# Graph attention whose row shifts are made by groups of tiles, without a common barrier before it, and whose late tiles wait for their own edge columns

## The chip, the cores and the metric

One Trainium2 chip, one of its cores. The metric is the device time of one execution in microseconds. A core has five instruction queues that run side by side and meet only by semaphores: PE (matrix products), DVE (vector), ACT (scalar, with function tables), POOL (GpSimd) and SP (here it only issues DMAs and reads registers).

## What is computed

Two layers of a graph network on 1250 nodes with 512 channels and 40000 edges. The part of the change is the sparse multi-head attention of the first layer (8 heads of 64):

```python
s = jnp.einsum('ehd,ehd->eh', q[src], k[dst]) / np.sqrt(D) + att_bias
m = jax.ops.segment_max(s, src, num_segments=n)
p = jnp.exp(s - m[src])
denom = jax.ops.segment_sum(p, src, num_segments=n)
alpha = p / jnp.where(denom[src] == 0, 1.0, denom[src])
agg = jax.ops.segment_sum(alpha[:, :, None] * v[dst], src, num_segments=n)
att = agg.reshape(n, C) @ Wo.T + bo
```

The edges come sorted by `dst`. The kernel works densely: `exp(q k - shift)` over all pairs of nodes, times a table in HBM that holds for each pair (dst, src) the sum of `exp(att_bias)` of its edges and their count. The shift of a source and head is its largest score over all nodes, with the sign turned and 40 added; any shift gives the same quotient.

## The kernel before

**Edge table.** Edge number n lies in column n // 128, 313 columns in all. `edges_pool` (from L610) adds one column after the other to the HBM table with an indirect DMA (L623), at most two in flight. The two semaphores `s_scat` count the landed even and odd columns. DVE makes the columns ready eight at a time ("turns": `mark` and `settle`, with PE's `spread_line` and `sum_repeats` and ACT's `copy_row`), a turn or two in each tile of the stages before. POOL does nothing but these scatters until they are all issued.

**Projections** (`gnn_pe`, `gnn_act`, `gnn_dve`, from L1101): ten tiles of 125 nodes, each with three products (q, k, v), their evictions on DVE (L1125), the transposes of q and k (copied by ACT, L1195 and L1196), and in the first six tiles two turns of edge work each. In tiles 0 to 4 PE spreads the first half of the next turn's keys before the transposes and the second half after them, which needs the first half copied by ACT (L412); ACT copies it behind the two copies of q and k. After the ten tiles DVE reads how many columns the first five tiles of `dst` need (`needed_columns_dve`, L644 to L647; the counting itself, L633 and L635, is in the tenth tile), adds the output bias to all ten tiles of `XN` (L1143), and builds constants (L1145 to L1154).

**Maxima.** 120 units of PE products (L1269) in four pairs of PSUM banks, each reduced by DVE (L1160): 12 units a tile, two of 512 columns and one of 226 for each of four pairs of heads. When all are done, DVE makes the shifts of all tiles (L1163, L1165), PE turns them (L1275), ACT copies them into `shiftT` (L1206), and PE, ACT and DVE call `leave_stage`, each waiting for the other two.

**Attention.** 50 blocks (5 chunks of 250 sources for the destination tiles 0 to 4, then again for tiles 5 to 9) of two units each, 100 units. For a unit, PE makes scores (L1550, L1556: the second adds the shift), ACT the exponentials in place (L1529, which needs the table of Exp), DVE multiplies them by the table's block (L1450), PE multiplies by the values (L1571), and a sum over a pass's weights is added up (L1486) by DVE in the first five passes and by POOL, behind the last scatter in its queue, in the other five. `att_sp` (from L1369) loads three blocks ahead into a ring of three slots (L223, L224, six DMAs and 1.1 MB each). Before the first it waits for the barrier, reads two registers (L651, L652) and waits for the columns that tiles 0 to 4 need (`soon_filled`); before block 25 it waits for all 313 (`table_filled`). Within a loop round i it waits for a_cc (counts copied), stores two small pieces of the adjacency, waits until block i is multiplied, and loads block i + 3. The place of the ring's third slot still holds edge values that the scatters read, so among the first 25 blocks the third of every three uses a slot of its own, `aside`.

## Time and profile before

| | us |
|---|---|
| median of 3 runs | 2275.96 |
| lowest and highest of them | 2274.62, 2282.95 |
| the profiled execution | 2270.11 |
| its span in the trace | 2268.0 |
| PE busy, DVE busy, ACT busy, POOL busy | 2064.1, 1348.2, 726.7, 730.7 |
| projections, about | 390 to 543 |
| maxima | 543 to 664 |
| between the last maximum and the first block multiplied | 664 to 679 |
| attention | 679 to about 1020 |

The profiled execution takes 2.1 us more than its span. The busy share of PE (91%) is a mean over stages: in the maxima and in the first half of the attention, PE waits for DVE. What an edit is worth is read from the waits of its own stretch. An instruction of POOL that issues a scatter is over when it is issued; its data land later. L-numbers are lines of the kernel before.

### The profile page before, as it was taken

How to read it: one execution, taken by the hardware profiler on the slowest of the kernel's cores; microseconds unless marked ns; L12 is line 12 of the kernel's file. 1: busy time of each engine (PE TensorE's matmuls, PEld its weight loads, DVE VectorE, ACT ScalarE, POOL GpSimd, SP SyncE). 2: the span in 40 equal slices, each digit the busy share in tenths (PEclk: the TensorE clock that was granted, in tenths of full speed). 3: DMA queues.
4: the chain of work that ended last, by engine and by line, in shares of the span. 5: the costliest groups of instructions: out<-in, count | busy, mean ns of one | idle time of the engine just before them, and what ended most of it. 6: DMA issues, size and time to landing. Idle time of an engine off the chain costs nothing.

```text
span 2268.0 us, 31396 instructions
## 1 busy us (share of the span) xinstructions
PE 2064.1 (91%) x11980; PEld 1260.4 (56%) x11980; DVE 1348.2 (59%) x3189; ACT 726.7 (32%) x1551; POOL 730.7 (32%) x508
## 2 busy tenths in 40 slices
PE   4998986888978898989999999999999999999977
PEld 3555554443325555546764457678677754455554
DVE  6665687877979997752224544341222243289997
ACT  4221122321015554422213355554111111135552
POOL 1346878887875635530000000000000000014443
PEclk9998998999999999999999999999999999999989
DMA  9994232223239987653000010004000014000000
GB/s 324 387 375 118 3 77 3 3 3 66 3 43 214 216 222 219 179 141 126 1 1 10 1 76 1 1 1 171 16 1 1 1 36 117 0 1 10 10 15 14
DMA packets 122053, 181.97 MB, mean 80 GB/s; under 512 B 67761, under 2 KB 69451, under 8 KB 118071
## 3 DMA queue, kind: packets, MB, share of 16 engines
q1 hardware_dynamic: 76833, 178.51, 24.9%
q0 software_dynamic: 45072, 1.46, 5.6%
q8 instruction: 95, 1.56, 0.3%
q14 instruction: 53, 0.43, 0.1%
HBM read 109.21 MB, written 70.71 MB: 79 GB/s over the span
## 4 chain that ended last, share of the span: by engine, by line
PE 58%; DVE 17%; POOL 11%; issue 5%; ACT 4%; DMA 3%; SPq 2%; DVEq 0%; PEldq 0%; ACTq 0%; POOLq 0%; PEld 0%
PE banks L204 17%; POOL edge_table L623 11%; PE banks L2400 6%; PE banks L2442 6%; DVE arena L1450 4%; PE banks L1751 3%; PE banks L2228 2%; PE banks L2216 2%; PE banks L2203 2%; PE banks L1550 2%; PE banks L2826 2%; DMA edge_table<-arena 2%; PE banks L2252 2%; PE banks L1571 2%; PE banks L198 2%
## 5 line engine op out<-in xcount | busy, mean ns | idle before, releaser
L623 POOL DMA_INDIRECT edge_table<-arena x313 | 525.4, 1678 | 256.6 <-DMA edge_table<-arena 153.6
L204 PE MATMUL banks<-arena 128*125 128x512 f32 x1200 | 554.9, 609 | 15.4 <-DVE arena L3046 14.3
L204 PEld LDWEIGHTS banks<-arena 128*125 128x125 f32 x1200 | 221.4, 193 | 261.1 <-issue 243.9
L2853 POOL CAST arena<-arena 125x128 f32<-125x128 uint32 x10 | 2.9, 292 | 699.3 <-DVE arena L2989 699.2
L1450 DVE TENSOR_TENSOR arena<-banks,arena 125x1000 f32<-125x1000 f32 x100 | 193.6, 1952 | 36.6 <-ACT banks L1529 19.7
L2348 DVE SCALAR_TENSOR_TENSOR arena<-banks,arena 125x512 f32<-125x512 f32 x80 | 60.1, 751 | 189.4 <-PE banks L2442 189.4
L2095 DVE CUSTOM_DVE_ANT_0 arena<-banks,arena 125x512 f32<-125x512 f32 (+8 forms) x144 | 73.0, 553 | 128.9 <-PE banks L2203 126.1
L2400 PEld LDWEIGHTS banks<-arena 128*128 128x128 f32 x1280 | 144.0, 192 | 6.7 <-issue 6.6
L1550 PE MATMUL banks<-arena 64*125 64x250 f32 x800 | 113.2, 402 | 37.1 <-DVE arena L1450 33.5
L2400 PE MATMUL banks<-arena 128*128 128x125 f32 x1280 | 146.4, 276 | 0.1
L2442 PE MATMUL banks<-arena 128*125 128x512 f32 x320 | 139.2, 593 | 0.0
L1529 ACT ACTIVATE banks<-banks 125x1000 f32<-125x1000 f32 x100 | 98.8, 988 | 123.4 <-PE banks L1556 117.2
L1486 POOL TENSOR_TENSOR arena<-arena 125x1000 f32<-125x1000 f32 x40 | 95.3, 2401 | 96.2 <-DVE arena L1450 96.2
L1269 PE MATMUL banks<-arena 64*125 64x512 f32 (+1 forms) x480 | 111.0, 564 | 8.0 <-DVE arena L1160 6.5
L1550 PEld LDWEIGHTS banks<-arena 64*125 64x125 f32 x800 | 69.2, 186 | 78.2 <-DVE arena L1450 54.1
L1160 DVE TENSOR_REDUCE arena<-banks 125x2 f32<-125x1024 f32 (+1 forms) x120 | 112.0, 1017 | 0.0
L2367 ACT ACTIVATE arena<-banks,arena 128x125 f32<-128x125 f32 x160 | 45.1, 368 | 203.2 <-PE banks L2400 203.2
L1571 PE MATMUL banks<-arena 125*64 125x250 f32 x800 | 107.3, 389 | 0.4 <-DVE arena L1450 0.4
L2061 POOL MEMSET arena<- 128x1250 f32 x1 | 1.1, 1141 | 315.7 <-PEq L148 315.7
L198 PE MATMUL banks<-arena 125*128 125x125 f32 x560 | 83.4, 281 | 21.3 <-DMA arena<-L_mix_Wv 6.7
L2442 PEld LDWEIGHTS banks<-arena 128*125 128x125 f32 x320 | 59.3, 188 | 74.0 <-issue 74.0
L198 PEld LDWEIGHTS banks<-arena 125*128 125x128 f32 x560 | 64.4, 145 | 52.5 <-issue 24.3
(372 smaller groups left out, 3394.0 us busy)
## 6 DMA issues: line engine op xcount, KB each, us to landing
edge_table<-arena SPq DMA_DIRECT2D x23, 2304.0 KB, 26.2
arena<-edge_table SPq DMA_DIRECT2D x100, 326.8 KB
arena<-edge_table SPq DMA_DIRECT2D x50, 330.8 KB
arena<-L_ffn_W SPq DMA_DIRECT2D x4, 2048.0 KB, 10.2
adjacency<-arena SPq DMA_DIRECT2D x50, 109.4 KB
arena<-adjacency SPq DMA_DIRECT2D x10, 546.9 KB
edge_table<-arena POOLq DMA_INDIRECT x313
arena<-edge_table SPq DMA_DIRECT2D x100, 37.9 KB
```

The lines of the kernel that those rows point to most:

```text
L198: last = nc.tensor.transpose(dst[:, k, :], src[:, k * 128:(k + 1) * 128], ident[0:TP, 0:TP])
L204: last = nc.tensor.matmul(dst, xT[:, i, :], w[:, i, 0:n], start=(i == 0), stop=(i == k - 1))
L623: pool.indirect_dma_start(d["table"], bass.IndirectOffsetOnAxis(ap=cell[0:EP, c:c + 1].bitcast(U32), axis=0), vals[0:EP, c * ROW:(c + 1) * ...
L1160: nc.vector.tensor_reduce(by_part_max[:, t, j, :, u % 3], both[:, :, 0:b - a], AX_X, ALU.max).then_inc(g_mx, 1)
L1269: last = nc.tensor.matmul(bank(2 * (u % 4) + e)[0:TP, 0:b - a], qT_g[64 * e:64 * e + 64, j, tok(t)], kT_g[64 * e:64 * e + 64, j, a:b], sta ...
L1450: nc.vector.tensor_tensor(weights_of(m).rearrange("p (s e n) -> p s e n", s=2, e=2), unit_scores(m).rearrange("p e (s n) -> p s e n", s=2) ...
L1486: ops.tensor_tensor(total_p, total_p, weights_of(m), ALU.add).then_inc(a_sum, 1)
L1529: nc.scalar.activation(unit_scores(m), unit_scores(m), ACT.Exp).then_inc(a_e, 1)
L1550: nc.tensor.matmul(bank(at + e)[0:TP, CHUNK * s:CHUNK * (s + 1)], kT_g[64 * e:64 * e + 64, 2 * h + s, tok(b)], qT_g[64 * e:64 * e + 64, 2 ...
L1571: last = nc.tensor.matmul(bank(h)[64 * e:64 * e + 64, CHUNK * s:CHUNK * (s + 1)], V_g[0:TP, b, DH * head:DH * (head + 1)], weights_of(m)[: ...
L2400: last = nc.tensor.matmul(bank(2 + n % 3)[:, m * TP:(m + 1) * TP], w1_e[a // 2][:, k, (c % 8) * 128:(c % 8 + 1) * 128], yT[:, k, tok(t)], ...
L2442: last = nc.tensor.matmul(bank(5 + n % 3)[0:TP, :], hT_e[t % 2][:, 2 * e + c, :], w2_e[e // 4][:, 2 * (e % 4) + c, :], start=(c == 0), sto ...
```

## The change

It touches five places.

1. **No barrier.** DVE, PE and ACT leave the stage with `pass_stage`, which counts and doesn't wait. SP no longer waits for the barrier. PE's first scores wait for the maxima that have read their banks instead; ACT loads the table of Exp with a dummy instruction.
2. **Shifts in three groups** (tiles 0 to 3, 4 to 7, 8 and 9). DVE makes a group's shifts right behind its last maximum; PE turns the first two groups four units later, in a pair of banks that is skipped for that round, and the last one behind the scores of units 0 and 1; the same on ACT.
3. **First blocks early.** SP waits only for the register values and for the columns of tiles 0 to 4, then loads blocks 0 to 2.
4. **Own columns for late tiles.** Four counts are made instead of one (for 5, 6, 7 and 8 tiles of `dst`). Blocks 25, 26, 27 wait for the columns of tile 5, 6, 7; block 28 waits for all. Blocks 26 and 29 go to `aside`.
5. **Work moved on DVE and ACT.** The counting goes from the tenth projection tile to the start of the first stage (behind `settle(dve, 0)`), the bias of `XN` from behind the ten tiles into each tile, and ACT copies the first half of the next turn's keys ahead of q and k.

```diff
@@ count_columns_dve, now called in mix_dve behind settle(dve, 0)
-            link(dve, nc.vector.scalar_tensor_tensor(out=away[0:EP, 0:USED], in0=key[0:EP, 0:USED], scalar=SOON_KEY,
-                                                     in1=pair_of[0:EP, 0:USED], op0=ALU.is_lt, op1=ALU.mult))
-            nc.vector.tensor_reduce(pairs_needed[0:EP, 0:1], away[0:EP, 0:USED], AX_X, ALU.max).then_inc(s_need, 1)
+            for w, key_bound in enumerate(SOON_KEYS):
+                link(dve, nc.vector.scalar_tensor_tensor(out=src_f[0:EP, 0:USED], in0=key[0:EP, 0:USED], scalar=key_bound,
+                                                         in1=pair_of[0:EP, 0:USED], op0=ALU.is_lt, op1=ALU.mult))
+                link(dve, nc.vector.tensor_reduce(pairs_needed[0:EP, w:w + 1], src_f[0:EP, 0:USED], AX_X, ALU.max))
+            nc.vector.tensor_copy(pairs_needed[0:EP, 4:8], pairs_needed[0:EP, 0:4]).then_inc(s_need, 1)
@@ soon_filled
+        def soon_filled(sp, w):
+            if w == 0:
+                sp.wait_ge(s_need, 4)
+            even = nc.sync.value_load(needed_even[:, w:w + 1], min_val=1, max_val=ALL_EVEN)
+            odd = nc.sync.value_load(needed_odd[:, w:w + 1], min_val=1, max_val=ALL_ODD)
             sp.wait_ge(s_scat[0], even)
             sp.wait_ge(s_scat[1], odd)
@@ gnn_dve
+                nc.vector.tensor_tensor(XN[0:TP, t, :], XN[0:TP, t, :], bo_g[0:TP, :], ALU.add)
             needed_columns_dve(dve)
-
-            for t in range(TILES):
-                nc.vector.tensor_tensor(XN[0:TP, t, :], XN[0:TP, t, :], bo_g[0:TP, :], ALU.add)
...
+                for group in SHIFT_TILES:
+                    if u + 1 == PER_TILE * group.stop:
+                        n = slice(HEADS * group.start, HEADS * group.stop)
+                        dve.wait_ge(g_mx, u + 1)
+                        link(dve, nc.vector.tensor_reduce(
+                            shift_g[0:TP, n], part_max[0:TP, :].rearrange("p (h c) -> p h c", c=3)[:, n, :], AX_X, ALU.max))
+                        nc.vector.tensor_scalar(shift_g[0:TP, n], shift_g[0:TP, n], -1.0, MARGIN, ALU.mult,
+                                                ALU.add).then_inc(g_shift, 1)
+            pass_stage(dve, "DVE")
@@ gnn_act
+                early = gnn_turns[t + 1][:-1] if t + 1 < TILES else ()
+                for k in early:
+                    copy_row(act, 2 * k)
                 act.wait_ge(g_tqk, t + 1)
...
+            for b in range(2):
+                copy_shifts(act, b)
+            nc.scalar.activation(degree_parts[0:TP, 63:64], ident[0:TP, 0:1], ACT.Exp)
+            pass_stage(act, "ACT")
@@ gnn_pe
+                for b_shift, at in enumerate(SHIFT_AT):
+                    if u == at:
+                        pe.wait_ge(g_mx, u - 3)
+                        turn_shifts(pe, b_shift)
+                    if u == at + 3:
+                        pe.wait_ge(g_shift, 3 * b_shift + 3)
@@ att_sp
-            sp.wait_ge(s_stage, 6)
-            soon_filled(sp)
+            soon_filled(sp, 0)
...
-                if i == BLOCKS // 2:
+                late = i - BLOCKS // 2
+                if 0 <= late < len(SOON_KEYS) - 1:
+                    soon_filled(sp, late + 1)
+                if late == len(SOON_KEYS) - 1:
                     table_filled(sp)
@@ att_pe
-            pe.wait_ge(g_shift, 3)
...
+                else:
+                    pe.wait_ge(g_mx, 1 + max(u for u in range(len(MAX_UNITS)) if 2 * pair_of_unit(u) == at))
+                if g < CHUNKS and n == 0 and h == 0:
+                    pe.wait_ge(g_shift, 3 * (tok(2 * c + 1).start // TP // 4) + 3)
```

On DVE, from the tenth projection tile's last eviction to the first block multiplied (the names in brackets are the semaphores that a row waits for), before:

```order
L1125 TENSOR_TENSOR arena<-banks,arena 125x512 [waits gnn_projected]
L644 TENSOR_REDUCE arena<-banks 1x1 [waits columns_needed_step]
L645 TENSOR_SCALAR arena<-arena 1x1 [waits dve_step]
L646 TENSOR_SCALAR arena<-arena 1x1 [waits dve_step]
L647 TENSOR_SCALAR arena<-arena 1x1
L1143 TENSOR_TENSOR arena<-arena 125x512 x10
...
L1160 TENSOR_REDUCE arena<-banks 125x2 [waits gnn_row_scores_ready] x120
L1163 TENSOR_REDUCE arena<-arena 125x80 [waits gnn_partial_maxima_ready]
L1165 TENSOR_SCALAR arena<-arena 125x80 [waits dve_step]
L1450 TENSOR_TENSOR arena<-banks,arena 125x1000 [waits att_exponentials_ready,table_block_loaded_0,stage_left]
```

and in the changed kernel:

```order
L1166 TENSOR_TENSOR arena<-banks,arena 125x512 [waits gnn_projected]
L1180 TENSOR_TENSOR arena<-arena 125x512
L650 TENSOR_REDUCE arena<-banks 1x4 [waits columns_needed_step]
...
L1197 TENSOR_REDUCE arena<-banks 125x2 [waits gnn_row_scores_ready] x48
L1203 TENSOR_REDUCE arena<-arena 125x32 [waits gnn_partial_maxima_ready]
L1205 TENSOR_SCALAR arena<-arena 125x32 [waits dve_step]
...
L1197 TENSOR_REDUCE arena<-banks 125x2 [waits gnn_row_scores_ready] x24
L1203 TENSOR_REDUCE arena<-arena 125x16 [waits gnn_partial_maxima_ready]
L1205 TENSOR_SCALAR arena<-arena 125x16 [waits dve_step]
L1488 TENSOR_TENSOR arena<-banks,arena 125x1000 [waits att_exponentials_ready,table_block_loaded_0]
```

Nine of the ten additions to `XN` have left this place, two of the three small shift pairs stand among the maxima, and the first multiplication no longer waits for the stage.

On SP, in front of the first block's six DMAs, before (`table_block_loaded` is what they raise):

```order
L1370 DMA arena<-L_gnn_Wo 128x2048 [waits repeats_summed]
L651 TENSOR_LOAD arena [waits columns_needed_step,stage_left]
L651 ISA x2
L652 TENSOR_LOAD arena
L652 ISA x2
L223 DMA arena<-edge_table 112x756 [waits columns_scattered_0,columns_scattered_1]
```

and in the changed kernel, there and in front of block 25 (the same stands in front of blocks 26 and 27):

```order
L1406 DMA arena<-L_gnn_Wo 128x2048 [waits repeats_summed]
L658 TENSOR_LOAD arena [waits columns_needed_step]
L658 ISA x2
L659 TENSOR_LOAD arena
L659 ISA x2
L223 DMA arena<-edge_table 112x756 [waits columns_scattered_0,columns_scattered_1]
...
L223 DMA adjacency<-arena 112x2x125 [waits att_counts_copied]
L224 DMA adjacency<-arena 13x2x125
L658 TENSOR_LOAD arena [waits att_weights_ready]
```

The wait for the stage is gone from the first read of a register, and pairs of such reads stand ahead of three late blocks.

On PE, between the last maximum's products and the attention's third unit, before:

```order
L1269 MATMUL banks<-arena 125x226
L1275 MATMUL banks<-arena 8x125 [waits gnn_shift_step]
L1275 MATMUL banks<-arena 8x125 x9
L1550 MATMUL banks<-arena 125x250 [waits gnn_shift_step,gnn_out_weights_loaded,stage_left]
...
L1621 MATMUL banks<-arena 125x512 x3
L1550 MATMUL banks<-arena 125x250 [waits att_weights_ready]
```

and in the changed kernel:

```order
L1311 MATMUL banks<-arena 125x226
L1593 MATMUL banks<-arena 125x250 [waits gnn_shift_step,gnn_partial_maxima_ready,gnn_out_weights_loaded]
...
L1081 MATMUL banks<-arena 8x125 [waits gnn_shift_step]
L1081 MATMUL banks<-arena 8x125
L1667 MATMUL banks<-arena 125x512 x3
L1593 MATMUL banks<-arena 125x250 [waits att_weights_ready]
```

The transposes of the shifts stood between the maxima and the scores; now only two of them are left, behind the first scores.

## Rows read from the trace of the kernel before

**Rows 1.** Timeline, 663 to 680 us: start, duration, engine, line; in brackets idle, releaser.

```profile
663.67 0.41 DVE L1163 TENSOR_REDUCE arena<-arena 125x80 f32<-125x240 f32 x1
...
664.36 1.49 PE L1275 MATMUL banks<-arena 125*8 125x125 f32 x10 [3.36 <-DVE arena L1165]
...
665.95 3.10 ACT L1206 ACTIVATE arena<-banks 8x500 bf16<-8x500 f32 x6 [122.85 <-PE banks L1275]
...
669.20 2.03 PE L1550 MATMUL banks<-arena 64*125 64x250 f32 x8 [3.34 <-ACTq L148]
...
671.05 0.32 SPq L223 DMA_DIRECT2D arena<-edge_table  x1
...
679.17 3.77 DVE L1450 TENSOR_TENSOR arena<-banks,arena 125x1000 f32<-125x1000 f32 x2 [14.87 <-DMA arena<-edge_table]
```

**Rows 2.** Waits of SP, 545 to 700 us: total, times, longest.

```profile
SPq L651 <- ACTq L148: 118.0, 1, 118.0
...
SPq L656 <- DMA edge_table<-arena: 0.4, 1, 0.4
```

**Rows 3.** Timeline of DVE from the last projection to the maxima.

```profile
541.94 6.09 DVE L1143 TENSOR_TENSOR arena<-arena 125x512 f32<-125x512 f32 x10
...
551.63 10.75 DVE L1160 TENSOR_REDUCE arena<-banks 125x2 f32<-125x1024 f32 x11
```

**Rows 4.** Groups by shape on DVE, 541 to 664 us: busy, mean ns, idle before.

```profile
L1160 DVE TENSOR_REDUCE arena<-banks 125x2 f32<-125x1024 f32 x80 | 93.9, 1216 | 0.0
L1160 DVE TENSOR_REDUCE arena<-banks 125x2 f32<-125x452 f32 x40 | 24.8, 620 | 0.0
```

**Rows 5.** Waits of DVE and of PE, 396 to 472 us, five projection tiles.

```profile
DVE arena L1125 <- PE banks L204: 14.6, 6, 6.0
...
PE banks L386 <- ACT arena L412: 9.1, 8, 1.6
```

**Rows 6.** Timeline of POOL: four of the 313 scatters.

```profile
655.13 1.54 POOL L623 DMA_INDIRECT edge_table<-arena  x1 [0.30 <-issue]
...
671.75 1.54 POOL L623 DMA_INDIRECT edge_table<-arena  x1 [0.30 <-issue]
...
687.07 1.54 POOL L623 DMA_INDIRECT edge_table<-arena  x1 [2.65 <-DMA edge_table<-arena]
...
804.23 1.54 POOL L623 DMA_INDIRECT edge_table<-arena  x1 [3.10 <-DMA edge_table<-arena]
```

**Rows 7.** Scatters by stretch: length, POOL busy (count), PEclk, DMA share, GB/s.

```profile
588.00:655.00 67.00, 55.48 (x36) 1.00 0.24 3
...
687.00:804.00 117.00, 67.40 (x38) 1.00 0.91 217
```

**Rows 8.** Waits of POOL, 687 to 804 us.

```profile
POOL edge_table L623 <- DMA edge_table<-arena: 45.1, 27, 3.8
```

**Rows 9.** Chain in order of time, a scatter's landing and block 31's.

```profile
584.12 3.94 DMA edge_table<-arena
...
851.26 4.06 DMA arena<-edge_table
```

**Rows 10.** Timeline of SP: first DMA of blocks 3, 28 and 31.

```profile
687.27 0.34 SPq L223 DMA_DIRECT2D arena<-edge_table  x1
...
831.83 1.85 SPq L223 DMA_DIRECT2D arena<-edge_table  x1
...
848.09 0.35 SPq L223 DMA_DIRECT2D arena<-edge_table  x1
```

**Rows 11.** Timeline of DVE and POOL: sums of DVE, unit 56, POOL's first sum.

```profile
690.18 1.20 DVE L1486 TENSOR_TENSOR arena<-arena 125x1000 f32<-125x1000 f32 x1
...
827.69 1.18 DVE L1486 TENSOR_TENSOR arena<-arena 125x1000 f32<-125x1000 f32 x1
...
841.65 1.98 DVE L1450 TENSOR_TENSOR arena<-banks,arena 125x1000 f32<-125x1000 f32 x1 [0.51 <-ACT banks L1529]
...
832.74 2.31 POOL L1486 TENSOR_TENSOR arena<-arena 125x1000 f32<-125x1000 f32 x1 [26.97 <-DVE arena L1450]
```

104 lines of the change are left out of this document (56 added, 48 removed).

## The prediction

> **What bounds the kernel now.** I read three views in this order: the timeline between the last maximum and the first block multiplied, the waits of SP and POOL, and the timelines of SP and DVE around the block where the change still waits for the whole table.
>
> Between the two stages stands a relay in which every engine waits for the one before it [rows 1]. DVE ends the maxima at 663.6 us and makes the shifts, PE turns them, ACT copies them for 3.1 us, the barrier opens, PE makes scores at 669.2, SP issues its first block at 671.05, and DVE multiplies at 679.17 after 14.87 us idle. From 663.6 to 679.17 are 15.5 us. The page's chain runs here through the scatters, which would say that SP waited for a column. SP's own waits say otherwise: 118.0 us at the first register read, released by ACT leaving the stage, and 0.4 us for columns [rows 2]. The barrier holds the loads, not the table.
>
> The maxima themselves are bound by DVE: 80 reductions of 1216 ns and 40 of 620 ns, with no idle time in front of them [rows 4], so what starts DVE earlier ends the stage earlier. Before them stand ten additions, 6.09 us in a row, on which nothing of this stage depends [rows 3].
>
> Beside all this POOL's queue of 313 scatters runs to 804.23 [rows 6]. While SP loads nothing, one scatter takes 67/36 = 1.86 us [rows 7]; with block loads beside it, from 687.07 to 804.23, 38 take 3.08 us each [rows 6], because POOL waits 45.1 us for earlier ones to land [rows 8] at a DMA share of 0.91 against 0.24 [rows 7]. The whole table must be landed before block 25 is loaded now, and before block 28 in the changed kernel. Now it just is; that is what I look at hardest.
>
> **Part by part.** *Projections.* In a tile with two turns PE waits about 1.65 us for ACT's copy of the keys (9.1 us in 8 waits, five of them long) [rows 5]; copied ahead of q and k, this wait goes. But DVE is nearly full there: apart from its first wait of 6.0 us it waits 14.6 - 6.0 = 8.6 us for PE in five tiles, 1.7 a tile [rows 5], and it gets a new addition of 0.61 (a tenth of 6.09) [rows 3]. So a tile can shorten by PE's 1.65 or by DVE's 1.7 - 0.6 = 1.1, whichever is less; in five tiles 5.0 us. The bounds are 0 and 8.2. What is queued behind the added work on DVE is the next tile's q eviction, for which PE's transposes wait.
>
> *Ten additions.* Nine leave the place in front of the maxima (5.5 us) and the tenth stays; reading four counts instead of one adds some 0.4. That is 5.1 us. The early counting, eight instructions on 313 columns, goes where DVE has nothing to do, while the first stage's weights arrive; I cost it at nothing, and 4 us if that cover were gone.
>
> *Shifts.* The one pair (0.41 and the next instruction [rows 1]) becomes three smaller ones; two stand among the reductions, 0.55 us each with their link, so 1.1 us more before the last maximum. The four transposes and the skipped bank pair leave PE two units ahead of DVE instead of three, which costs nothing as long as DVE has no idle time [rows 4]. The bounds are 0 and 2 us.
>
> *The relay.* The first scores need only the first group's shifts and banks that are free three reductions before the end. Exp's table is loaded early. Blocks 0 to 2 were issued some 65 us before. So DVE's first multiplication follows the last shift pair: I take 0.9 us after the last maximum (0.4 for the pair, the rest for its link and the drain) instead of 15.5. That is 14.6 us. PE doesn't rest before it, so its scores run at full clock: eight products took 2.03 us after the pause, and the third unit was late; I take 0.7 us for that.
>
> Unhindered, the attention so moves forward by 5.0 + 5.1 - 1.1 + 14.6 + 0.7 = **24.3 us**.
>
> *The table's end.* The scatters don't move forward. They are slowed twice. First, the three early blocks are loaded beneath the maxima, as soon as the columns of tiles 0 to 4 are in (about 588). The same three loads now cost the scatters from 671.75 to 687.07 four intervals in 15.3 us instead of 7.4 [rows 6]: **7.9 us lost**, the nearest row there is. Second, the regular loads begin 24.3 us earlier, at 687.27 - 24.3 = 663.0 [rows 10], and from then on a scatter takes 3.08.
>
> Count them. The scatter issued at 655.13 [rows 6] is number 262 of 313; with 7.9 us lost it is issued at 663.0. SP wants block 28 at 831.83 - 24.3 = 807.5 [rows 10]. From 663 to 808 are 145 us, 47 scatters, so number 309. Four are left. SP stands at its gate and loads nothing, so they go at 1.86: the last is issued at 815.4 and lands 3.94 later [rows 9], at 819.4. Then block 28 is loaded. Block 31 took from its issue at 848.09 [rows 10] to 851.26 + 4.06 = 855.3 [rows 9], 7.2 us, so block 28 is there at 826.6 and unit 56 is multiplied at **826.7**. Unhindered it would be 841.65 - 24.3 = 817.4 [rows 11]. DVE stands still for about 9 us, and 841.65 - 826.7 = **15 us** are left of the 24.
>
> POOL's sums are behind the same scatters. They begin at 817 (832.74 now, 2.31 each [rows 11]); unit 55 needs the first of them, at 819.3, and unit 56 the second, at 821.6. Both are earlier than the block, so they add nothing. The gates of blocks 25 to 27 (columns 243 to 281, by 802 at the latest) are open long before; the register reads ahead of them cost SP 1 to 2 us, which the ring's lead covers (9.8 us from issue to use for block 28, less 7.2).
>
> The 15 us hardly depend on the first terms. If the attention started 4 us later, the loads would slow two scatters fewer and the last would still land near 819. What sets the result is the scatter queue: at a busy pace of 3.18 instead of 3.08, 1.5 scatters more are left at 808, which costs 1.5 x 1.86 = 2.7 us.
>
> Against the profiled execution (2270.11, span 2268.0) this gives a span of 2253 and 2255 us. The profiled execution was 5.9 us under the median of the three runs; taking 15 off the median 2275.96 gives **2261**.
>
> **A rule weighed.** Why are scatters slower beside the attention? In the rows they wait for landings, and POOL's own time per scatter rises only from 55.48/36 = 1.54 to 67.40/38 = 1.77 us [rows 7]. The Trainium skill ("SBUF — State Buffer", SBUF: two separate sides) says that DMA and engine accesses cannot slow each other, but that DVE and GpSimd share a port pair under an exclusive lock, held for a whole instruction by a DVE operation with two SBUF inputs. By that rule DVE's sums, not the loads, would be the brake. That is the first rival.
>
> **Rivals.** (a) *The early blocks cost the scatters nothing, and the gate is open in time.* If only DVE's sums slow the scatters, the brake acts from 690.18 - 24.3 = 665.9 to 827.69 - 24.3 = 803.4 [rows 11]. By 665.9, number 267 is issued, 137.5 us later number 312, and the last lands at 808, half a microsecond after SP wants block 28. No stall is left and the gain is the full 24: **2252**. Against it: between 671.75 and 687.07 the scatters were slow while DVE made no sums [rows 6, 11]. Chance 0.12, with other ways to a timely end.
>
> (b) *The end of the table is later.* If the last four don't speed up (3.08 each, 12.3 us instead of 7.4) and land as late as two intervals of the busy pace, 6.2 us instead of 3.9, the gate opens 7 us later and 8 us of gain remain: **2268**. For it: SP's stop frees the queue only after block 27 has landed. Against it: scatters keep 1.86 for 36 in a row when no load runs [rows 7]. Chance 0.22.
>
> (c) *Slower than before.* The same gate, from the point where block 28 is issued after 834.5 (7.2 us before 841.65). That is 15 us later than I take it, 8 scatters more at 1.86, and so a busy pace of 145/39 = 3.7 us. At 4.0, 36 scatters are issued by 808 and 11 more are left, the gate opens 20 us later, and the kernel loses 5 us: **2281**. For it: the scatters and the loads together hold 0.91 of the DMA engines [rows 7]. Against it: the loads come at the same rhythm as now. Chance 0.06.
>
> (d) *It doesn't do what it says*: another semaphore brings back the relay. SP would then show a long wait at its first read again. By the listed order nothing is left there to wait for; it is in (b)'s chance.
>
> **The numbers.** Forecast 2261 with chance 0.60 (gains of 11.5 to 20 us). About 0.5% (11.4 us) is what a measurement of this kernel can tell from no change, so faster means under 2264.6: 0.60 + 0.12 = 0.72. Within 0.5%: (b) and a little of (c), 0.23. Slower: 0.05. The range 2250 to 2270 holds the forecast with a pace of 2.9 to 3.3 and an early-load cost of 5 to 10 us, most of (a), and (b) with a gain of 8.
>
> **What would show it.** Right: SP's wait at its first register read is gone and its first block is issued near 588; the first multiplication stands within 2 us of the last shift pair, at about 655; four or five scatters are missing against the quiet pace behind 588; DVE waits 7 to 11 us for a block at unit 56, near 817 to 827, and SP waits for the scatters' landing just before. Wrong: no such wait at unit 56 (rival a), a first multiplication later than 660 (the projection term, or a bank released late), or a wait at unit 55 for POOL's sums. The forecast fails most easily in the busy pace of the scatters.

## The result, and the profile after

The changed kernel takes **2259.37 us** (median of 5 runs, 2256.33 to 2264.42) against 2275.96 of the kernel before on the same chip, 5 runs as well: ratio **0.9936**, 95% interval 0.9915 to 0.9957. The two medians alone would give 0.9927, inside that interval. The forecast was 2261. On another chip the same pair gave 0.9951 (0.9934 to 0.9969; 2259.28 against 2271.29). The profiled execution took 2257.32 us, its span is 2255.5, with a granted clock of 0.977 (0.975 before). Compared with the profiled execution of before, the first block is multiplied 28.4 us earlier, and the last of the 100 units only 13.4 us earlier. The document is about the 15 us between.

Line numbers have moved: maxima L1160 is now L1197, block products L1450 L1488, sums L1486 L1524, ACT's gather L1510 L1548 and exponential L1529 L1567, PE's scores L1550 L1593. Units and scatters are numbered from 0, and *the first multiplication* is DVE's of unit 0.

The relay between the stages [rows 1] is gone. Timeline of DVE, after (start, duration, engine, line, operation; in brackets idle time and its releaser):

```profile
636.89 12.95 DVE L1197 TENSOR_REDUCE arena<-banks 125x2 f32<-125x1024 f32 x14
649.87 0.20 DVE L1203 TENSOR_REDUCE arena<-arena 125x16 f32<-125x48 f32 x1
650.11 0.41 DVE L1205 TENSOR_SCALAR arena<-arena 125x16 f32<-125x16 f32 x1
650.73 3.81 DVE L1488 TENSOR_TENSOR arena<-banks,arena 125x1000 f32<-125x1000 f32 x2 [0.21 <-issue]
```

From the last maximum to the first multiplication are 0.9 us, where 15.5 were. SP's wait at the first register read [rows 2] is gone too; in its place SP waits for columns, twice. Waits of SP, 545 to 850 us (total, times, longest):

```profile
SPq L664 <- DMA edge_table<-arena: 38.9, 1, 38.9
SPq L668 <- DMA edge_table<-arena: 13.5, 1, 13.5
```

The first (L664, the columns of tiles 0 to 4) ends at 581.8 and delays nothing behind it: the blocks are there long before they are used. The second (L668, the whole table, in front of block 28) stands where the forecast looked for it, from 802.5 to 816.0. Waits of DVE, 650 to 850 us:

```profile
DVE arena L1488 <- ACT banks L1567: 16.1, 12, 5.7
DVE arena L1488 <- POOL arena L1524: 7.0, 1, 7.0
```

and the same place in the timelines of DVE (units 54 to 57) and POOL (last scatter, first sums):

```profile
807.83 1.95 DVE L1488 TENSOR_TENSOR arena<-banks,arena 125x1000 f32<-125x1000 f32 x1
816.78 1.94 DVE L1488 TENSOR_TENSOR arena<-banks,arena 125x1000 f32<-125x1000 f32 x1 [7.00 <-POOL arena L1524]
824.43 3.79 DVE L1488 TENSOR_TENSOR arena<-banks,arena 125x1000 f32<-125x1000 f32 x2 [5.71 <-ACT banks L1567]
...
812.88 1.54 POOL L623 DMA_INDIRECT edge_table<-arena  x1 [0.33 <-issue]
813.88 9.62 POOL L1524 TENSOR_TENSOR arena<-arena 125x1000 f32<-125x1000 f32 x4
```

DVE stands still twice: at unit 55, whose buffer comes free only with POOL's first sum, and at unit 56, for block 28. Both waits go back to POOL's last scatter. The chain of waits, in order of time, follows it:

```profile
812.88 3.07 DMA edge_table<-arena
815.96 0.02 SPq L668
...
816.01 0.32 SPq L223
...
818.02 4.62 DMA arena<-edge_table
...
822.67 0.03 ACT arena L1548
```

The last scatter lands (3.07 us), SP passes its gate, issues block 28, whose last part is in flight for 4.62 us more, and ACT gathers from it. In numbers: up to unit 54 the attention runs 29.3 us ahead of before, at unit 56 17.2 us. **12.1 us of the lead are lost at two units**, and 3.8 more by unit 66.

### The profile page after: what moved, and what is told of

It reads as the page before. It is cut to its first block, busy times and chain, and to the rows that moved or that the text cites. A ratio compares the mean times of both kernels' runs of the same rounds, so it can differ in the third digit from the quotient of the medians.

```text
span 2255.5 us, 31449 instructions
## 1 busy us (share of the span) xinstructions
PE 2059.9 (91%) x11986; PEld 1259.6 (56%) x11986; DVE 1352.0 (60%) x3200; ACT 728.0 (32%) x1552; POOL 726.3 (32%) x508
## 4 chain that ended last, share of the span: by engine, by line
PE 59%; DVE 17%; DMA 9%; POOL 7%; ACT 4%; issue 3%; SPq 1%; DVEq 0%; PEldq 0%; ACTq 0%; POOLq 0%; PEld 0%
PE banks L204 17%; DMA edge_table<-arena 8%; POOL edge_table L623 7%; PE banks L2446 6%; PE banks L2488 6%; PE banks L1797 3%; PE banks L2274 2%; PE banks L2262 2%; PE banks L2249 2%; PE banks L2872 2%; PE banks L1593 2%; PE banks L2298 2%; PE banks L198 2%; PE banks L1614 1%; DVE arena L1488 1%
## 5 line engine op out<-in xcount | busy, mean ns | idle before, releaser
L1488 DVE TENSOR_TENSOR arena<-banks,arena 125x1000 f32<-125x1000 f32 x100 | 193.3, 1949 | 35.5 <-ACT banks L1567 26.9
L1593 PE MATMUL banks<-arena 64*125 64x250 f32 x800 | 113.8, 403 | 38.6 <-DVE arena L1488 37.3
L1567 ACT ACTIVATE banks<-banks 125x1000 f32<-125x1000 f32 x100 | 99.0, 990 | 139.9 <-PE banks L1599 120.1
L1524 POOL TENSOR_TENSOR arena<-arena 125x1000 f32<-125x1000 f32 x40 | 95.8, 2455 | 74.3 <-DVE arena L1488 74.2
L1593 PEld LDWEIGHTS banks<-arena 64*125 64x125 f32 x800 | 69.3, 187 | 79.9 <-DVE arena L1488 58.0
L1197 DVE TENSOR_REDUCE arena<-banks 125x2 f32<-125x1024 f32 (+1 forms) x120 | 112.2, 1029 | 0.0
## 6 DMA issues: line engine op xcount, KB each, us to landing
edge_table<-arena SPq DMA_DIRECT2D x23, 2304.0 KB, 24.3
arena<-L_ffn_W SPq DMA_DIRECT2D x4, 2048.0 KB, 10.1
```

The lines of the kernel that those rows point to most:

```text
L1197: nc.vector.tensor_reduce(by_part_max[:, t, j, :, u % 3], unit_banks(u)[:, :, 0:b - a], AX_X, ALU.max).then_inc(g_mx, 1)
L1488: nc.vector.tensor_tensor(weights_of(m).rearrange("p (s e n) -> p s e n", s=2, e=2), unit_scores(m).rearrange("p e (s n) -> p s e n", s=2) ...
L1524: ops.tensor_tensor(total_p, total_p, weights_of(m), ALU.add).then_inc(a_sum, 1)
L1567: nc.scalar.activation(unit_scores(m), unit_scores(m), ACT.Exp).then_inc(a_e, 1)
L1593: nc.tensor.matmul(bank(at + e)[0:TP, CHUNK * s:CHUNK * (s + 1)], kT_g[64 * e:64 * e + 64, 2 * h + s, tok(b)], qT_g[64 * e:64 * e + 64, 2 ...
```

## The experiments

Two theories were to be told apart. **The queue**: the end of the 313 scatters sets when block 28 and POOL's sums come, so behind unit 56 nothing depends on when the attention began. **The start**: each microsecond of an earlier start counts, and the shortfall is elsewhere. A third question was what slows the scatters: the block loads or DVE's sums.

All profiles beside each other; the times in microseconds are read from the timelines, the ratios are timed runs against the kernel before on the same chip. The variants were timed on three chips, and the changed kernel itself again on one of these, beside *barrier back*, *projections back* and *306 scatters*. The half-widths of the intervals are 4 to 7 us, so small differences are read only together with a profile.

| kernel | first multiplication | last scatter issued | unit 56 | unit 99 | ratio, 95% |
|---|---|---|---|---|---|
| before | 679.2 | 804.2 | 841.6 | 992.6 | 1 |
| after | 650.7 | 812.9 | 824.4 | 979.2 | 0.9936 (0.9915-0.9957) |
| after, again | 650.0 | 815.9 | 827.3 | 981.4 | 0.9951 (0.9934-0.9969) |
| barrier back | 653.9 | 818.9 | 830.5 | 982.3 | 0.9928 (0.9900-0.9956) |
| first loads late | 658.4 | 815.2 | 827.2 | 981.6 | 0.9928 (0.9897-0.9959) |
| projections back | 666.5 | 809.5 | 827.8 | 979.0 | 0.9944 (0.9922-0.9966) |
| gate at block 25 | 651.1 | 811.1 | 839.9 | 992.9 | 0.9984 (0.9968-1.0001) |
| gate at block 29 | 649.4 | 819.4 | 825.6 | 984.3 | 0.9946 (0.9926-0.9966) |
| sums from unit 56 | 648.0 | 818.7 | 829.6 | 983.7 | 0.9938 (0.9915-0.9960) |
| both of these | 650.3 | 819.5 | 812.8 | 978.9 | 0.9950 (0.9931-0.9968) |
| 306 scatters | 649.0 | 806.1 | 818.0 | 971.8 | 0.9894 (0.9870-0.9918) |
| 288 scatters | 653.7 | 745.4 | 814.8 | 968.4 | 0.9880 (0.9852-0.9908) |
| thin loads | 648.5 | 770.8 | 809.7 | 962.3 | one execution, 2240.16 us |
| unused products | 650.7 | 817.2 | 828.8 | 995.4 | 1.0016 (0.9999-1.0034) |

### Does the start matter? Three ways to start later

*Projections back.*

```diff
-                nc.vector.tensor_tensor(XN[0:TP, t, :], XN[0:TP, t, :], bo_g[0:TP, :], ALU.add)
             needed_columns_dve(dve)
+            for t in range(TILES):
+                nc.vector.tensor_tensor(XN[0:TP, t, :], XN[0:TP, t, :], bo_g[0:TP, :], ALU.add)
```

(and ACT copies the early turn behind q and k again)

> The changed kernel without its edits to the projections: nine of the ten additions stand in a row before the maxima again, and ACT copies the early turn behind q and k. The maxima and with them the first multiplication come about 12 us later (662 instead of 650.7). My theory (the queue sets the end): the scatters run as before, SP wants block 28 at about 813.5 and gets it at 816 to 822; unit 56 is at 162 to 168 us from the first multiplication, unit 99 at 315 to 322, so at 977 to 984 in all as in the changed kernel, and the time is that of the changed kernel within 3 us (or some microseconds better, since DVE's pauses get shorter). Rival (the start sets the end): 12 us slower than the changed kernel, a ratio near 0.999 to the kernel before.

The attention starts 16.5 us later than in the changed kernel's second profile beside it, and unit 99 comes 2.4 us **earlier**; the ratios are the same. Timeline of DVE, units 56 and 57 of this kernel:

```profile
827.83 1.98 DVE L1489 TENSOR_TENSOR arena<-banks,arena 125x1000 f32<-125x1000 f32 x1 [0.51 <-ACT banks L1568]
830.49 1.98 DVE L1489 TENSOR_TENSOR arena<-banks,arena 125x1000 f32<-125x1000 f32 x1 [0.69 <-ACT banks L1568]
```

There is no stall: DVE idles 0.51 us in front of unit 56, where 5.71 stood, and SP has no wait at its gate for the whole table. From its first multiplication to unit 99 this kernel takes 312.5 us (less than the 315 to 322 that I had expected), the kernel before 313.4, the changed kernel 328.5 and 331.5.

*Barrier back.*

```diff
-            pass_stage(dve, "DVE")
+            leave_stage(dve, "DVE")
...
```

(and the same for ACT and PE)

> The changed kernel with DVE, ACT and PE waiting for each other at the end of the first stage again; SP still loads the first blocks near 588. DVE's first multiplication comes 3 to 4 us after the last shift pair instead of 0.3, for PE makes its scores only behind the barrier. My theory (the queue): these 3 to 4 us are lost at the start and given back at units 55 and 56, the time is that of the changed kernel within 2 us. Rival (the start sets the end): 3 to 4 us slower, a ratio of 0.995 to 0.996.

The first multiplication comes at 653.86, 3.3 us after the last shift instruction, and unit 99 at 982.3, against 979.2 and 981.4 in the two profiles of after; the ratio, 0.9928, isn't worse than that of the changed kernel. A shift of 3 us is no larger than what two profiles of one kernel differ by, so this kernel alone would decide little.

*First loads late.*

```diff
             sp.dma_start(wo_g.rearrange("p k n -> p (k n)"), d["L0_gnn_Wo"]).then_inc(s_wo_g, 16)
+            sp.wait_ge(s_stage, 6)
             soon_filled(sp, 0)
```

> The changed kernel, where SP loads the first three blocks only when all engines have left the first stage (about 651) instead of near 588; no other engine waits. The first multiplication so comes about 8 us later (block 0 there at 658 to 660). My theory (the queue): scatters no longer lose 8 us near 588, lose about as much behind 651, and the last lands within 2 us of 816 as before; block 28 is wanted at 811, is there at 822 to 824, and unit 56 starts within 2 us of 824.4. The span stays at 2253 to 2257, though the attention began 8 us later. Rival (the start of the attention sets the end): each microsecond of the start counts, span 2263 to 2264.

The start is 7.7 us later than in the first profile of after, unit 56 2.8 and unit 99 2.4 us later; against the second profile they are equal within 0.2. The ratio is that of the changed kernel. The span of this profile, 2260.2, lies between my 2253 to 2257 and the rival's 2263 to 2264, but 2.3 to 2.8 us of its excess arise behind unit 99, outside this stage. Against the second profile of after the start moved by 3.9, 8.4 and 16.5 us in the three kernels, and unit 99 by 0.8, 0.2 and -2.4. The theory of the start has fallen, by *projections back* above all.

### Is it the queue? Three kernels with less of it

*288 and 306 scatters.*

```diff
-            for c in range(USED):
+            for c in range(288):
...
-        ALL_EVEN, ALL_ODD = 16 * -(-USED // 2), 16 * (USED // 2)
+        ALL_EVEN, ALL_ODD = 16 * 144, 16 * 144
```

(the same in the wait for the whole table; 306 and 153 in the other)

> The changed kernel with the last 25 of the 313 scatters left out (the rows of those columns are missing from the table, so the output differs); all waits for the whole table count 288. Nothing else is changed. My theory (the queue): the changed kernel lost 12.1 us at units 55 and 56 because the last scatter lands at about 816, and 3.8 us more in the units behind, where PE works at half clock after its pauses. With 288 scatters the last lands near 750 and SP wants block 28 at about 802. So there is no wait for scatters in front of block 28, none of DVE for POOL's sums, unit 56 is multiplied at 815 instead of 824.4, and the span is about 16 us under 2255.5, near 2240; against the kernel before a ratio near 0.987. Rival (the ring of blocks or ACT limits the units behind 800 anyway): the wait moves, but units 64 to 99 come no more than 3 us earlier, and the span stays above 2252. Rival (the start sets the end, the shortfall is the noise of one execution): nothing changes, 2255.

Both waits are gone, unit 56 is at 814.83 (in its timeline the DVE row shows 0.50 us idle), the span is 2244.5 (11 us under 2255.5, not the 16 that I had expected), and the timed ratio 0.9880 is 13 to 16 us better than the two of the changed kernel (0.0056 and 0.0071 of 2270).

> The changed kernel with the last 7 of the 313 scatters left out (their rows are missing from the table, so the output differs), all counts 306. My theory (a threshold: the queue costs only what it is later than SP's wish for block 28 near 802 and DVE's for the first sum near 809): the last scatter is issued between 795 and 805, and nearly the whole cost goes, 10 to 14 of the 14 to 16 us that leaving out 25 gave; ratio to the kernel before 0.987 to 0.990, unit 99 at 315 to 320 from the first multiplication. Rival (each scatter costs its share of time, through its traffic): 7/25 of that, 4 to 5 us, ratio 0.992.

A threshold, as expected: leaving out 7 scatters of 313 gives 0.9894, 9.5 to 13 us better than the changed kernel, most of what 25 give. Each of the two differences is known to about 7 us; against the changed kernel on the same chip (13 us) the rival's 4 to 5 us are outside, against the first (9.5 us) they are not. The profile missed what I had expected (last scatter 806.1, unit 99 at 322.8 us from the first multiplication). This execution still had a rest of the stall, for here the queue was late (its scatters number 225 and 305 came 6 and 11 us later than in the first profile of after). Timelines of POOL and DVE:

```profile
806.11 1.55 POOL L623 DMA_INDIRECT edge_table<-arena  x1 [0.30 <-issue]
...
810.03 1.95 DVE L1488 TENSOR_TENSOR arena<-banks,arena 125x1000 f32<-125x1000 f32 x1 [2.11 <-POOL arena L1524]
817.96 3.79 DVE L1488 TENSOR_TENSOR arena<-banks,arena 125x1000 f32<-125x1000 f32 x2 [5.98 <-ACT banks L1567]
```

It took 2260.0 us, the longest of its six, and lost 10 us behind unit 99, outside this stage; the median is 2247.8, against 2259.28 of the changed kernel on that chip.

### What slows the scatters?

```diff
                 for v, w in BLOCK_PARTS:
-                    spread(sp, edge_block(i)[0:TP, v:w, :], table[tok(b), c * CHUNK + v:c * CHUNK + w, :], s_tab[i % RING])
+                    few = w if i < RING or i >= BLOCKS // 2 else v + 4
+                    spread(sp, edge_block(i)[0:TP, v:few, :], table[tok(b), c * CHUNK + v:c * CHUNK + few, :], s_tab[i % RING])
```

> The changed kernel with blocks 3 to 24 loaded only in part: each of their transfers carries 4 source columns instead of 83 or 84, with as many DMAs and the same semaphores (most of the data of these blocks is left out, so the output differs). Blocks 0 to 2 and 25 to 49 are loaded whole. DVE, ACT, PE and POOL do the same work. My theory (the loads are the brake): behind 663 the scatters keep about the quiet pace of 1.85 us instead of 3.18, the last is issued near 750, and block 28 meets an open gate. Rival (DVE's sums with two SBUF inputs are the brake, through the port that DVE and POOL share): the sums are still there, so the pace stays near 3.1 to 3.2 between 663 and 800 and DVE waits 8 us and more at unit 55 or 56. Between the two (2.3 to 2.8) both would have a part. Span about 2240 by my theory, 2252 to 2256 by the rival.

POOL from 663 to 800 us (length, busy and count, granted clock, DMA share, GB/s), after and then thin loads:

```profile
663.00:800.00 137.00, 75.31 (x44) 1.00 0.93 214
```

```profile
663.00:800.00 137.00, 84.19 (x51) 1.00 0.42 55
```

DVE's sums in the same stretch, after and then thin loads (groups by shape: busy, mean ns, idle before):

```profile
L1524 DVE TENSOR_TENSOR arena<-arena 125x1000 f32<-125x1000 f32 x39 | 46.6, 1196 | 0.0
```

```profile
L1526 DVE TENSOR_TENSOR arena<-arena 125x1000 f32<-125x1000 f32 x38 | 45.5, 1196 | 0.0
```

The whole blocks come back near 790, so the second row understates the difference: from 663 to 765 us it is 34 GB/s against 220. With the same sums, as many DMAs and nearly as many load packets in these 102 us (12756 against 13145), but a sixth of the bytes per second, scatters 270 to 310 come every 2.14 us ((765.4 - 679.6) / 40), and all are issued by 770.8. In after, 44 in 137 us are 3.11 each. So the loads' bytes bring about 1.0 of the 1.25 us by which a scatter is slower than the quiet 1.86 [rows 7]. DVE's sums are not the main cause. I had expected 1.85, and the 0.3 left have two parts: POOL's own instruction is 0.12 us longer on average, and it idles 0.18 us more between two, which stays open between the adjacency stores and the thin loads themselves. POOL waits for landings, in after and with thin loads (663 to 800 us):

```profile
POOL edge_table L623 <- DMA edge_table<-arena: 55.6, 27, 4.9
```

```profile
POOL edge_table L623 <- DMA edge_table<-arena: 11.7, 12, 2.0
```

POOL's own part is where DVE is seen. A scatter's instruction takes 1.54 to 1.56 us wherever DVE makes no operation with two inputs from SBUF (once 1.66, beside memsets and casts), block loads or not. A scatter issued just behind the start of one of DVE's sums is longer, with thin loads:

```profile
690.28 1.21 DVE L1526 TENSOR_TENSOR arena<-arena 125x1000 f32<-125x1000 f32 x1
690.39 2.52 POOL L623 DMA_INDIRECT edge_table<-arena  x1 [0.30 <-issue]
```

and the kernel before has a scatter that lasts through its ten additions [rows 3], from 543.22 to 549.45, though none of the block loads runs then:

```profile
543.22 6.23 POOL L623 DMA_INDIRECT edge_table<-arena  x1 [0.30 <-issue]
```

With the additions back (*projections back*) one takes 5.00 us at the same place; in after, all from 540 to 580 us take 1.54. The Trainium skill ("SBUF — State Buffer", SBUF: two separate sides) describes such a lock between DVE and GpSimd, and the trace agrees with it for these instructions; as the brake of the attention's scatters, which the prediction weighed, it accounts for 0.1 to 0.2 us of each. The Trainium skill ("DMA: Bandwidth & Descriptors", SWDGE vs HWDGE vs iDMA) says that each DMA engine takes its queues in turn; a scatter's small packets would then stand behind the large ones of a load. The longer landings agree with that; single packets were not followed.

### Where the gate and the sums stand

*Gate at block 25* (the last part of the change undone).

```diff
-                if 0 <= late < len(SOON_KEYS) - 1:
-                    soon_filled(sp, late + 1)
-                if late == len(SOON_KEYS) - 1:
+                if late == 0:
                     table_filled(sp)
```

> The changed kernel without its last part: block 25 waits for the whole table as in the kernel before, blocks 26 to 49 wait for nothing. My theory (the queue): SP wants block 25 near 786, when some 11 scatters are still to be issued; while it stands they go at 1.85 us, the last lands at about 811, block 25 is there at 818.5, and DVE stands still for about 20 us at unit 50, then waits no more for POOL's sums. Unit 56 comes at about 831 instead of 824.4, the span is 5 to 8 us longer than the 2255.5 of the changed kernel: 2261 to 2263. Rival (the landing hardly moves because the gate frees it): the last scatter lands so much earlier that the span is within 2 us of the changed kernel's. Rival (the start sets the end): 2255.

The whole gain is gone, 0.9984. DVE waits once, at unit 50:

```profile
822.31 1.93 DVE L1486 TENSOR_TENSOR arena<-banks,arena 125x1000 f32<-125x1000 f32 x1 [25.85 <-ACT banks L1565]
```

I had expected 20 us here, unit 56 at 831 and a span of 2261 to 2263; they were 25.85 us, 839.9 and 2268.0. The mistake: SP stopped 18 us sooner than at block 28, but the last scatter came only 1.8 us sooner than in the first profile of after (811.1 against 812.9), since at 785 the queue was further behind there (299 scatters issued against 302, and 300 in the second profile of after). The gates of single tiles are thus worth 7.5 to 11 us (each known to about 6), most of what the change brings as a whole.

*Gate at block 29, sums from unit 56, and both.*

```diff
-        SOON_KEYS = [float((SOON_TILES + w) * TP * NODES + 1) for w in range(4)]
+        SOON_KEYS = [float(w * TP * NODES + 1) for w in (SOON_TILES, SOON_TILES + 2, SOON_TILES + 3, SOON_TILES + 4)]
...
-                if late == len(SOON_KEYS) - 1:
+                if late == 4:
                     table_filled(sp)
```

```diff
-                if m >= 1 and place(m - 1)[1] and place(m - 1)[0] < DVE_PASSES:
+                if m >= 1 and place(m - 1)[1] and m - 1 < POOL_FROM:
                     sum_weights(nc.vector, dve, m - 1)
```

(`POOL_FROM` is 56, and POOL makes the sums from there on)

> The changed kernel with another choice of gates: block 25 waits for the columns of tiles 0 to 6, block 27 for tile 7, block 28 for tile 8, and only block 29 for the whole table. My theory (the queue sets the end, and the loads slow it): SP isn't stopped at block 28 but loads it near 802, so the scatters keep the busy pace some 5 us longer, the last is issued near 815 and lands near 818.5, block 29 is there at 826. Unit 56 no longer waits for its block, but unit 55 waits for POOL's first sum at 818.5 and the next ones follow at POOL's pace of 2.3 us, so unit 58 starts at 826 instead of 830. Counted from the first multiplication, unit 99 comes at 324 to 325 us instead of 328.5: 4 us faster than the changed kernel. Rival (the landing moves with the gate, microsecond for microsecond): less than 1 us is gained. Rival (only the wait for block 28 costs anything): 10 us and more are gained, unit 99 at 318 or less.

> The changed kernel where DVE makes the sums of units 52 to 55 as well, and POOL starts at unit 56; the gates are those of the changed kernel. My theory (block 28 ends last): unit 55 starts near 811 instead of 816.8, its 7 us of waiting for POOL's sum are gone, but unit 56 still waits for block 28 until 824.4; DVE's wait for ACT in front of it grows from 5.7 to about 11. Unit 99, counted from the first multiplication, stays within 1.5 us of 328.5. Rival (POOL's sums are the cost, the block comes second): unit 99 comes 5 us earlier or more.

> Both at once: only block 29 waits for the whole table, and POOL's sums start at unit 56. My theory (the last scatter's landing near 818.5, then the load of block 29, ends last): unit 56 starts near 815 to 817, unit 58 waits for block 29 until 826; unit 99 within 1.5 us of what the other gates alone give, 323 to 325 from the first multiplication. Rival (with the other gates POOL's sums end last): 3 us and more are gained beyond the other gates alone, unit 99 at 321 or less.

DVE's rows at the stall, with the gate at block 29 (unit 55), with the sums from 56 (unit 56):

```profile
823.33 1.94 DVE L1488 TENSOR_TENSOR arena<-banks,arena 125x1000 f32<-125x1000 f32 x1 [15.32 <-POOL arena L1524]
```

```profile
829.62 1.92 DVE L1489 TENSOR_TENSOR arena<-banks,arena 125x1000 f32<-125x1000 f32 x1 [19.01 <-ACT banks L1568]
```

The two waits are in parallel: take one away and the other grows by about as much. With both edits, unit 56 is at 812.8 as if there were no queue, and then DVE stands 13.50 us for block 29 at unit 58. The timed ratios, 0.9938 to 0.9950, are no better than the changed kernel's. The 4 us that I had expected of the later gate did not come: from the first multiplication to unit 99 it took 335.0 us, 335.7 with the sums alone and 328.5 with both (328.5 and 331.5 in the changed kernel). So the profiles of the first two missed what I had expected by 7 to 11 us, and the one with both is 6.4 us shorter than with the gate alone, which the timed ratios (0.9950 and 0.9946) don't repeat. In all three the last scatter was issued at 818.7 to 819.5, 3 to 7 us later than in after. For the gate at 29 a part of that was expected, as the loads go on longer, but with the sums alone nothing touched the queue before 800; how much is the edit and how much the execution was not separated. No variant that computes everything beat the changed kernel by more than the intervals.

### The same kernel again, and PE's clock

> The changed kernel again, unchanged, on the same chip as the three runs beside it. In its first profile the last scatter was issued at 812.9; in the profiles of the variants that don't touch the queue before 800 it was issued between 815.2 and 819.4, with the first multiplication at 648.0 to 653.7. If the first profile was a lucky one (my theory now), the last scatter comes at 815 to 819 here, and unit 99 at 331 to 335 us from the first multiplication instead of 328.5. Rival (the variants delay the queue): 812 to 814 and 328 to 329 again. The ratio to the kernel before stays within 0.9915 to 0.9957 either way.

The last scatter came at 815.9 instead of 812.9, DVE waited 11.1 us for POOL's sum instead of 7.0, and the attention took 331.5 us instead of 328.5. So the first profile was a good one for the queue: its scatter number 225 was issued at 582.4, those of the other variants between 583.9 and 588.9, though all but one run the same instructions until then.

*Unused products.*

```diff
+                if m == 55:
+                    pe.wait_ge(a_r, CHUNKS)
+                    unused_products(bank(3), wo_g[:, 0, :], 26)
+                if m == 56:
+                    unused_products(bank(3), wo_g[:, 0, :], 12)
                 if m + 2 < UNITS:
                     scores(m + 2)
```

> The changed kernel with unused products of 512 columns on PE in its two pauses: 26 in front of the scores of unit 57, 12 in front of those of unit 58 (one constant matrix into a bank that nobody reads then; the results are not used). My theory (besides the wait, the pause costs a slow clock behind it): the granted clock doesn't fall behind 812, the scores of units 57 to 59 take 1.1 us for eight products instead of 1.8 to 2.0, and unit 66 comes 1 to 3 us earlier, counted from unit 56. Unit 56 itself stays where it is. Rival (the lateness behind unit 56 comes from block loads that land just in time): the clock is kept but units 58 to 66 stay as late, within 0.5 us. Rival (the fillers get in the way): unit 57 starts later than now.

The rival of the products that get in the way was right: one of them is two rows in the trace and takes 0.86 us, so that the first 26 held PE until 834.4, and the kernel became 15 to 18 us slower. Timeline of PE:

```profile
811.88 22.48 PE L210 MATMUL banks<-arena 128*128 128x512 f32 x52
```

The clock did stay at 1.00, but what that is worth can't be read from this kernel. It is read from other profiles. PE by stretch in the second profile of after:

```profile
808.00:812.00 4.00, 3.33 (x28) 1.00 0.23 2
812.00:816.00 4.00, 0.00 (x0) 0.75 0.24 2
816.00:820.00 4.00, 0.00 (x0) 0.50 0.27 7
820.00:824.00 4.00, 2.24 (x12) 0.50 0.95 274
...
832.00:836.00 4.00, 4.00 (x26) 0.69 0.61 157
836.00:840.00 4.00, 4.00 (x38) 1.00 0.88 238
```

PE is without work from 812 to 820, and then the granted clock is 0.50 (1.2 GHz) until about 834. From unit 56 to unit 59 the two profiles of after take 10.1 and 9.5 us, the kernel before and the one with 288 scatters 7.6. So the slow clock behind the stall costs 2 to 2.5 us there, or less if another wait has a part in it; with the barrier back, where it ends sooner, it is 1.0 us.

It falls a second time, 25 us later, and there with 288 scatters and with thin loads too. PE by stretch, and the rows of PE and DVE in front of unit 66, in after and then before:

```profile
853.00:857.00 4.00, 4.00 (x22) 0.57 1.05 262
...
854.08 1.93 PE L1614 MATMUL banks<-arena 125*64 125x250 f32 x8
...
857.74 0.68 DVE L1463 TENSOR_TENSOR arena<-banks,arena 128x500 f32<-128x500 f32 x1 [2.40 <-PE banks L1653]
```

```profile
867.00:871.00 4.00, 3.56 (x28) 1.00 1.02 297
...
868.70 1.06 PE L1571 MATMUL banks<-arena 125*64 125x250 f32 x8
...
871.13 0.68 DVE L1425 TENSOR_TENSOR arena<-banks,arena 128x500 f32<-128x500 f32 x1 [0.81 <-PE banks L1608]
```

The same products take 1.93 us instead of 1.06, DVE waits 2.40 us for PE instead of 0.81, and 1.6 us are lost. All profiles fall into two kinds: from unit 64 to unit 66 it is 6.2 us (before, projections back, barrier back, the kernel with both late gate and sums, unused products) or 7.7 to 7.8 (all others). PE waits 2.4 us for DVE in front of these products in either kind; why the clock falls in one and not in the other is open.

## Why the prediction was right, and where it wasn't

**The mechanism was right, and it is shown**: the gain is what the end of the scatter queue leaves over, not what the start wins. Leaving out part of the queue brings 9.5 to 16 us; starting 4 to 16 us later costs nothing that can be measured. The sentence that the result hardly depends on the first terms held to a degree that I had not dared: all edits to the projections together are worth nothing that can be measured here.

**Term by term.** *Projections:* 5.0 predicted. From the first to the last copy of a turn (L412, 30 of them) ACT takes 131.4 and 130.3 us in the profiles of after, 138.7 in before and 138.6 again with the edit undone: 7.3 to 8.3, at the upper bound of 8.2. I had let DVE's 1.7 us a tile limit it; PE's wait was the measure. *Additions:* 5.1 predicted; the maxima start 14.8 us earlier, of which 7.3 are the projections and 2.8 a lead that this execution had before them (first L412 of the projections at 386.4 against 389.1; at 384.9 to 389.0 in the other profiles of changed kernels, so the early counting costs nothing that is seen), which leaves 4.8. *Shifts:* 1.1 against 1.0 (the maxima take 113.0 us instead of 112.0). *Relay:* 14.6, exact. *PE at full clock:* 0.7 predicted, 1.4 (the step from unit 0 to unit 4 takes 10.8 us instead of 12.1). Together 29.8 at unit 4 and not 24.3, of which 2.8 came before the edited stretch.

*Early loads:* 7.9 predicted. Timeline of POOL, scatters 225 and 232:

```profile
582.39 1.54 POOL L623 DMA_INDIRECT edge_table<-arena  x1 [0.30 <-issue]
...
603.17 1.54 POOL L623 DMA_INDIRECT edge_table<-arena  x1 [0.30 <-issue]
```

Seven intervals in 20.8 us instead of 13.0: **7.8 us**, and 6.9 to 9.0 in the other profiles with early loads. DVE made only reductions from banks and one small shift pair then, none of its sums. This is the same price as in [rows 6], and a second place where the loads alone slow the queue. *Busy pace:* 3.08 predicted; (805.48 - 662.51) / 45 = 3.18 here (scatters 263 to 308, counted from 0; the prediction counts from 1). *SP's wish for block 28:* 807.5 predicted, 802.5, earlier by the larger lead. *Reads of registers:* 1 to 2 us predicted, 1.5 in front of block 25 (784.6 to 786.1). *Last scatter:* 815.4 predicted, 812.9 and 815.9 measured; landing 3.94 predicted, 3.07; block 28 from issue to use 7.2 predicted, 822.67 - 816.01 = 6.7. Unit 56 at 826.7 predicted, 824.4 and 827.3 measured.

**What the sum lacked or had wrong.** *POOL's sums:* I let unit 55 wait until 819.3 in the sum, but wrote that they "add nothing", and named a wait at unit 55 for POOL's sums as a sign of being wrong. That sign came: they hold DVE 7.0 and 11.1 us at unit 55, the longer of the two waits, and the wait for the block at unit 56 is 5.7 and 5.6 us, not 7 to 11. The two together, 12.7 in the first profile, are the stall of about 9 that I had put at unit 56 alone. Beyond the block the sums do add nothing, and the kernel with DVE's sums shows it (0.9938), but anyone who opens only the gate finds them behind it. *Behind unit 56* I had taken the lead as kept. It shrinks by 3.8 us more: 2.2 up to unit 64, behind the stall and its slow clock, and 1.6 up to unit 66 by the second slow stretch. With 288 scatters it still shrinks by 2.6 (unit 56 is 26.8 us ahead of before, unit 99 24.2): 1.0 by unit 64, with a wait for a block in front of unit 60, and the same 1.6; with thin loads 0.1 and the same 1.6. So PE's clock, of which the sum knew nothing behind the stall, takes most of this. These losses and the larger start nearly cancel, and that is luck: so 15 us of gain in the forecast stand beside 11.1 and 13.4 in the profiles at unit 99, and 14.6 and 11.1 in the timed pairs.

**The rivals.** (a), no stall, fell with both of its halves: the early loads do cost the scatters 7.8 us, and with DVE's sums in place and thin loads the pace falls to 2.14. The port that it rests on is real, but small here. (b), a gate that opens 7 us later than the 819.4 of the forecast, did not happen in either profile (816.0 and 819.0); its lesser form is seen: in executions with the same queue the last scatter was issued anywhere from 812.9 to 819. (c), slower, needed a pace of 3.7 over that stretch; 3.2 was the slowest seen. (d) is refuted by SP's waits.

## What to carry to other kernels

When a stage is made to start earlier, look for the queue that does not start earlier and has to be done within it. Here the start could move at least 12.7 us (projections back: 679.2 to 666.5, no stall, unit 99 at 979.0) before it met the end of the scatters, and all of the further 16 us (650.7 instead of 666.5) were lost. Past that point work on the queue: a few entries of it can be worth as much as a whole rewrite of what stands before. 7 of 313 scatters were worth about 11 us. And where two waits hang on one landing, removing one of them shows nothing; take both away, or the landing.

## What the runs showed of the hardware that I had not expected

Indirect scatters are slowed by the bytes of the loads beside them, not by the number of DMAs: as many DMAs at 34 GB/s instead of 220 (663 to 765 us) let a scatter pass in 2.14 us instead of 3.11. When the loads stop, the quiet pace is there with the next scatters (805.48, 807.33, 809.17 in after).

An indirect scatter's own instruction on POOL, 1.54 us, is held up beside DVE operations with two inputs from SBUF: it took 2.52 us beside one sum, 6.23 and 5.00 beside ten additions in a row. Beside DVE's multiplications, which read a bank and SBUF, it took 1.54 to 1.56.

Behind the same wait of 2.4 us for DVE, in front of the products of units 64 to 66, PE's granted clock fell to 0.57 over 4 us in after and stayed at 1.00 in before. The fall cost 1.6 us, in nine of the fourteen profiles.

Two executions of the same instructions differ by several microseconds in where such a queue stands: scatter 225 came at 582.4 to 588.9 and the first multiplication of kernels with the same work ahead of it at 648.0 to 653.7, not in step. A difference of 3 us between two single profiles of this kernel proves nothing.
